# A gated delta recurrence between two mixtures of experts on one core: the passes in a loop, one product instead of two, setup work moved

## The reference, cut to what matters

```python
x = L0_attn_x                                             # 4 x 1024 tokens, 256 wide
x = x + 0.5 * ffn(layernorm(x), w1, w2, router_w)         # 8 experts, top 2
x = x + attn(layernorm(x), Wq, Wk, Wv, ...)               # 8 heads of 32
x = x + 0.5 * ffn(layernorm(x), w1, w2, router_w)

# attn, for each token: a decay g, a write that removes, and a write that adds
bS = einsum('bhk,bhkv->bhv', b_t, S)
S = exp(g)[..., None] * S + a_t[..., None] * bS[:, :, None, :] + k_t[..., None] * v_t[:, :, None, :]
o = einsum('bhk,bhkv->bhv', q_t, S)
```

## Time and profile before

| what | value |
|---|---|
| median of 3 runs | 1948.43 us |
| the profiled execution's own time | 1948.43 us |
| its span, first to last instruction | 1946.6 us |
| busy share of PE, PEld, DVE, ACT, POOL | 78%, 66%, 60%, 40%, 38% |
| granted clock of TensorE, mean | 0.866 of full speed |
| instruction blocks read by DMA | 52 of 0.85 MB together, 51 of 0.42 MB together |

### The profile page before, as it was taken

How to read it: one execution, slowest core, us unless ns; L and a number is a source line. 1 busy time by engine, 2 the same in 40 slices (tenths; PEclk the granted TensorE clock), 3 DMA queues, 4 the chain that set the end, 5 groups by cost and what they waited for, 6 DMA issues and landing times. The chain is left out here.

```text
span 1946.6 us, 68464 instructions
## 1 busy us (share of the span) xinstructions
PE 1526.0 (78%) x26124; PEld 1288.5 (66%) x26125; DVE 1163.2 (60%) x3492; ACT 779.9 (40%) x1805; POOL 747.1 (38%) x944
## 2 busy tenths in 40 slices
PE   5499999998566478664787647777467799999995
PEld 5499999998245365352654526545355699999994
DVE  7546444443287776777767786767956346444442
ACT  1243333332376234672345732356433343333331
POOL 2554422222075251671514725228344123522221
PEclk9999999999678587785777866978768899999998
DMA  9554322222101000010000001000100653333324
GB/s 308 181 160 87 74 49 46 47 48 41 57 7 47 23 22 22 5 49 23 22 22 3 32 29 30 26 2 17 36 12 22 217 159 59 81 68 49 49 48 109
DMA packets 84231, 116.20 MB, mean 60 GB/s; under 512 B 12952, under 2 KB 74464, under 8 KB 82016
## 3 DMA queue, kind: packets, MB, share of 16 engines
q1 hardware_dynamic: 56224, 76.27, 12.6%
q0 software_dynamic: 27360, 37.80, 10.9%
q10 hardware_dynamic: 544, 0.86, 0.1%
HBM read 64.87 MB, written 54.21 MB: 61 GB/s over the span
## 5 line engine op out<-in xcount | busy, mean ns | idle before, releaser
L1059 POOL DMA_INDIRECT x<-ffn_yout,ffn_place x142 | 222.5, 1567 | 531.4 <-DVE ffn_yout L991 455.2
L997 DVE TENSOR_TENSOR ffn_inner<-ffn_inner,ffn_bank 128x512 f32<-128x512 f32 x142 | 97.6, 687 | 348.0 <-PE ffn_bank L871 345.6
L871 PE MATMUL ffn_bank<-ffn_tileT,ffn_gate_now 128*128 128x128 f32 x2272 | 279.3, 276 | 0.0
L871 PE MATMUL ffn_bank<-ffn_tileT,ffn_up_now 128*128 128x128 f32 x2272 | 276.9, 275 | 0.0
L881 PE MATMUL ffn_bank<-ffn_w,ffn_inner 128*128 x1136 | 268.9, 380 | 1.7 <-DVE ffn_yout L991 1.7
L952 ACT ACTIVATE ffn_inner<-ffn_bank 128x512 f32<-128x512 f32 x142 | 84.8, 597 | 458.2 <-PE ffn_bank L871 458.1
L871 PEld LDWEIGHTS ffn_bank<-ffn_tileT,ffn_gate_now 128*128 128x128 f32 x2272 | 267.6, 193 | 0.1
L871 PEld LDWEIGHTS ffn_bank<-ffn_tileT,ffn_up_now 128*128 128x128 f32 x2272 | 265.1, 192 | 0.0
L881 PEld LDWEIGHTS ffn_bank<-ffn_w,ffn_inner 128*128 128x128 f32 x1136 | 205.0, 190 | 24.4 <-issue 2.5
L814 ACT COPY ffn_gate_now<-ffn_w 128x1024 f32 x142 | 148.4, 1045 | 29.3 <-issue 22.1
L814 DVE COPY ffn_up_now<-ffn_w 128x1024 f32 x142 | 99.4, 700 | 54.5 <-issue 43.4
(11 more groups left out here) (493 smaller groups left out, 3112.1 us busy)
## 6 DMA issues: line engine op xcount, KB each, us to landing
ffn_w<-in_w1t_dram SPq DMA_DIRECT2D x16, 1024.0 KB, 5.5
ffn_tile<-xs SPq DMA_DIRECT2D x122, 130.0 KB, 2.1
ffn_w<-in_w2t_dram SPq DMA_DIRECT2D x16, 512.0 KB, 6.4
ffn_x<-in_x_dram SPq DMA_DIRECT2D x16, 256.0 KB, 5.3
x<-ffn_x SPq DMA_DIRECT2D x16, 256.0 KB, 5.7
pass_xa<-x SPq DMA_DIRECT2D x12, 256.0 KB, 3.6
pass_xr<-x SPq DMA_DIRECT2D x12, 256.0 KB, 2.7
x<-pass_xr SPq DMA_DIRECT2D x12, 256.0 KB, 2.1
```

What stands on the lines that cost most here:

```text
L871: t = pe.matmul(bank[:, i * P:(i + 1) * P], half_now[half][b][:, k, i * P:(i + 1) * P], rowsT[b][:, k * P:(k + 1) * P], start=(k == 0), st ...
L997: dve.tensor_tensor(inner[b][:, :], inner[b][:, :], p_u[b][:, :], ALU.mult).then_inc(s_act, 1)
L1059: pool.indirect_dma_start(total, bass.IndirectOffsetOnAxis(ap=place[b][:, 0:1], axis=0), yout[b][:, :], None, compute_op=ALU.add).then_inc ...
```

## The change

There are four edits.

1. In `setup_scalar` the two waits for the rows of x are gone; the transfers of `wq`, `wv` and `wo` follow the three small ones.
2. The first three passes become one body in a loop over all five engines (`nc.Fori`), with the pass number in a register. The last pass stays outside. Everything that depended on the number (row addresses of the transfers, the count that GpSimd waits for in `invert`) takes it from the register. Tiles are called `pass_...` in either program here.
3. In `between`, `setup.vector_end` is called at the end of VectorE's part instead of ahead of `log_f`.
4. In the triangle stage two products of GpSimd, each for one of two interleaved columns, become one with a further dimension.

```diff
--- before.py
+++ after.py
@@ -1163,8 +1163,6 @@
             act.dma_start(wrank[0:RANK, :], w["wf2"]).then_inc(s_w, 16)
             act.dma_start(wrank[RANK:2 * RANK, :], w["wog2"]).then_inc(s_w, 16)
             act.dma_start(wrank[2 * RANK:FG, :], cst["negsel"]).then_inc(s_w, 16)
-            for h in range(2):
-                act.wait_ge(s_x[h], 16 * BATCH // 2)
             for dst, src in ((wq, "wq"), (wv, "wv"), (wo, "wo")):
                 act.dma_start(dst[:, :, :], w[src]).then_inc(s_w, 16)
             act.wait_ge(s_init, 1)
@@ -1244,8 +1242,8 @@
             between(nc, sb, sem, psum, None, 0, env, {"o": None, "xr": None, **first_rows}, routing, setup)
             clear(nc, sems)
         begin.close()
-        for s in range(PASSES - 1):
-            one(f"pass{s}", s, s + 1)
+        with nc.Fori(0, PASSES - 1) as s:
+            one("pass", s, s + 1)
         one("end", PASSES - 1, None)
         clear(nc, kept)
 
@@ -1539,8 +1537,6 @@
                     r.logits_vector(dve, 0)
                     r.choose_vector(dve, 0, lambda: log_f(3))
                 elif begins:
-                    if setup is not None:
-                        setup.vector_end(dve)
                     for j in range(4):
                         log_f(j)
                 if begins:
@@ -1552,6 +1548,8 @@
                         dve.wait_ge(s_kn, j + 1)
                         dve.wait_ge(s_bb, j + 1)
                         dve.tensor_tensor(both(kb, g, c), both(k, g, c), psum[4 + j][:, :], ALU.mult).then_inc(s_kb, 1)
+                if setup is not None:
+                    setup.vector_end(dve)
 
 
 def decays_and_triangles(nc, sb, sem, psum, s, env, last=False):
@@ -1729,10 +1727,8 @@
                         pool.tensor_tensor(out[:, :, 0:4].rearrange("p n (a r) -> p n a r", r=2), kf2.unsqueeze(2).to_broadcast([P, NB, 2, 2]), both, ALU.mult)
                         pool.tensor_tensor(out[:, :, 6:8], planes([]), two(kb, c)[:, :, 1:2].to_broadcast([P, NB, 2]), ALU.mult)
                         pool.wait_ge(s_lt, n + 1)
-                        for s, first in ((0, kf2), (1, two(k, c))):
-                            i = pool.tensor_tensor(out[:, :, 8:12].rearrange("p n (a s) -> p n a s", s=2)[:, :, :, s],
-                                                   first[:, :, 0:1].to_broadcast([P, NB, 2]), late2, ALU.mult)
-                        i.then_inc(s_pr, 1)
+                        pool.tensor_tensor(out[:, :, 8:12].rearrange("p n (a s) -> p n a s", s=2), planes([[0, 2]]),
+                                           late2.unsqueeze(3).to_broadcast([P, NB, 2, 2]), ALU.mult).then_inc(s_pr, 1)
                         if n + 1 < CHAINS:
                             pool.wait_ge(s_pr, n + 1)
```

## The result

The changed kernel took 1961.69 us (median of 6 runs, 1958.24 to 1970.90); the kernel before, on the same chip, 1946.70 us (6 runs, 1931.10 to 1952.44). The ratio is 1.0106, 95% interval 1.0063 to 1.0149: 12 to 29 us more. I had forecast 1946.6 us, and 1939.5 to 1954.5 us as the range.

The account below looks back on a forecast made before the run. No engine bounds the whole kernel; GpSimd was taken to set the triangle stage. Product -9.6, setup +2.5, weights +1.4 and jumps +3.9 summed to -1.8 us, 1948.4 to 1946.6 us; range 1939.5 to 1954.5 us.

Parts of the forecast that it names:

- The merged product: Triangle stage, GpSimd: one product of 1.32 us replaces a pair of 1.61 us, 9.6 us less over four passes.
- planes: Merged product's first operand, read by planes far apart: 0.075 us extra on 256 elements, so 0.15 us on 512.
- my upper bound of 1.70: Merged product's dearest case, running like two of L1723 (0.850 us, strided operands): a loss of 0.09 us a chain.
- rival 3: Triangle stage, GpSimd: the single product is no cheaper than the pair; 1952.3 us, slower; chance 0.15.
- its 1.60 us: Merged product by the skill page's rule for reads stepping over 8 bytes: 1.175 + 0.43 us, saving nothing.
- The end of the stage follows GpSimd: Triangle stage: GpSimd's last product sets its end, so ending 2.4 us earlier shortens each pass by that.
- 0.5 us to spare: Triangle stage: room left for VectorE's last keys once GpSimd ends 2.4 us earlier; savings above 0.36 us a chain cut off.
- Setup work last, +2.5: Before the first pass: VectorE's setup work, moved behind its last keys, is covered by nothing; +2.5 us once.
- Weights early, +1.4: Start: the three weight transfers share the DMA engines with x, whose last half megabyte lands later; +1.4 us.
- The jumps, +3.9: Loop's two jumps back: VectorE's late instruction block costs 2.44 us, of which 1.95 show, twice; +3.9 us.
- rival 2: Loop's jumps: ScalarE's head is fetched as well, +4.9 instead of 3.9 us, 1947.6 us; chance 0.16.
- my 9.8 us bound: Loop's jumps, upper bound: two late blocks in a row for every engine, 4.9 us at each jump.

## Why the prediction was wrong

**The merged product: the step that failed.** I took 1.175 us from L1729 "since L1729 is the nearest in shape" and added 0.15 us for planes: 1.32 us, a gain of 0.29 a chain. It took 1.846 us: 0.24 more than the pair, above my upper bound of 1.70. The pace went from 5.71 to 6.00 us, so 32 x 0.29 = 9.3 us were lost where 9.6 were to be won: 19 us of error, more than the whole difference between forecast and result. Neither operand alone predicts it: with either one still it took 1.17 us, so the planes that I priced at 0.15 us cost nothing by themselves; with both moving, 1.85. L1729, the row that I argued from, has one operand that returns to the same two neighbours. Of my bounds, the upper one came from one long operand pattern (L1723), and no row of before showed two at once; that deserved a wider bound and rival 3 a larger chance than 0.15. A smaller slip: two operations of 0.805 us are 1.61, but the earlier trace rows has 12.5 us busy for 8 pairs, 1.56 us a pair. That is why the product at 1.31 us, nearly my own figure, brought GpSimd's end forward by 8.2 us in all, 0.26 and not 0.30 a chain. The trace agrees with the direction of the Trainium skill's rule that I set aside (GPSIMD Engine Reference, section 7): its 1.60 us was nearer than mine. But the rule names the step alone, and with the same far step at every element the product took 1.31 us in another order (row, token, column); here the runs decide.

**The end of the stage follows GpSimd.** Right, and it held in both directions: +7.4 to +9.7 us with a slow product; with the one at 1.31 us GpSimd ended 8.2 us earlier over the four stages, and the stages were 10.9 us shorter; the 2.7 us beyond that are luck with TensorE's clock. The keys, which I gave 0.5 us to spare, came last in one of the four stages there.

**Setup work last, +2.5.** Right: 2.8 us, a little above my bound of 2.6, and nothing came back.

**Weights early, +1.4.** Right in mechanism (x's second half late, the first not). In size the edit alone made x 2.1 us late and the stage 1.4 us longer, too little to tell from the spread; that it equals my figure is luck. With the setup edit beside it x was late by 2.35 to 3.20 us, past my bound of 2.2.

**The jumps, +3.9.** The stage was right, the engines were not. I had VectorE's block late and the blocks of ScalarE and GpSimd "probably" kept, with 2.44 us of which 1.95 show. VectorE and ScalarE both start late, by 3.2 to 4.0 us a jump, 6.5 to 8 us in all. That is rival 2, with more than one block's price; my 9.8 us bound holds it. From the earlier trace rows, where TensorE kept three blocks in a loop of 210 instructions, I concluded that ScalarE's 213 and GpSimd's 96 of a pass would stay too; those rows are of another engine, and for ScalarE the conclusion didn't hold. For GpSimd it stays open: its first operation starts 0.5 us after ScalarE starts the factor, with the loop and without, so a late block of its own would not show. The rule of the Trainium skill that I weighed (Runtime: NRT & Kernel Launch, Instruction fetch mechanics: a taken branch out of the two held pages has to fetch its target) agrees with ScalarE's 7.33 us on issue, where the rows of TensorE's short loop had pointed the other way. I had set those rows against it wrongly: the same section gives TensorE four times the instruction memory of most engines, so a loop that TensorE keeps doesn't speak against it.

**The sum.** -9.6 + 2.5 + 1.4 + 3.9 = -1.8 was forecast; +9.3 (product) + 2.8 (setup) + 2.3 (weights) + 6.5 (jumps) = +21 is what the terms measured, each at its own place. By whole stages of the same profiles it is +9.7, +5.1 and +3.7, together 18.5 of the 20 us between the two profiles: the stretches ahead of the looped passes grew by less than the jumps, within the 2.6 us by which untouched ones differ. The timed interval of 12 to 29 holds both sums. With the product's term put right (the whole change, token innermost) the stages give -9.6, +6.1 and +4.6, together +1.1 us, and the ratio was 1.0006.

## What to carry to other kernels

Price a merged elementwise operation on GpSimd by a row in which *both* operands move as in the new one; if there is none, let the bounds reach past the dearest row, and try the orders of its axes, since the same 512 products cost 1.31 to 1.86 us. The loop here, a whole pass long, paid a block fetch at the head of every further iteration on VectorE and ScalarE at once, behind a barrier where nothing hid it; look at what stands first after the jump. Compare stages, not totals: edits worth 5 to 8 us each were plain in their stages and could not be told from nothing in twelve timed runs. And read TensorE's clock at the end of a stage before a microsecond of it is put down to an edit.

## What the runs showed of the hardware that I had not expected

- GpSimd, 128x512 f32 product of two operands: 1.17 us with one operand still inside each four elements, 1.31 us with the row outermost and 1.41 us with the column outermost, 1.85 us when both operands jump in a four-element cycle.
- The same 128 matmuls at the end of a triangle stage took 2.78 us at the lower clock (0.50 granted) and 1.7 us at full clock, in two passes of one execution.
- A jump back over a whole pass cost 3.2 to 4.0 us on VectorE and ScalarE; a hint on the branch took it down to 0.2 to 0.8 us. In both hinted kernels TensorE then stopped for 3.1 and 3.6 us behind the loop's end.
- 768 KB of weights on ScalarE's queue, sent beside 1 MB of x on SyncE's, made the second half of x 2.1 to 3.2 us late, against 0.05 to 1.2 us in kernels that held them back.
